# One ring of three PSUM banks for the two softmax attention cores of an eight-sublayer kernel

## What is computed

```python
# layer 0: 16 heads of 32. The last 16 context rows are "compressed" (DCA): own key and value
# projections, and a softmax of their own beside that over the other 496 rows
out = softmax(q k_main^T * s) v_main + DCA_WEIGHT * softmax(q k_dca^T * s) v_dca
# layer 3: 32 heads of 16, rotary embedding on q and k, one softmax over all 512 rows
w = softmax(einsum('bhqd,bhkd->bhqk', q, k) * scale); attn = einsum('bhqk,bhkd->bqhd', w, v)
```

## Time and profile before

| what | value |
|---|---|
| median of 3 runs (lowest to highest) | 3214.14 us (3209.91 to 3215.42) |
| time of the profiled execution | 3215.47 us |
| its span in the trace | 3213.7 us |
| layer 0's attention core | 235.8 to 566.0 us of the span |
| layer 3's attention core | 2333.6 to 2757.3 us of the span |
| TensorE matmul, VectorE, ScalarE, GpSimd busy | 77%, 68%, 50%, 35% |

### The profile page before, as it was taken

The page is one execution under the profiler, slowest core; times in us unless marked ns, Lnnn a source line. Parts: engine busy times, 40 slices in busy tenths (PEclk is TensorE's granted clock), DMA queues, the critical chain, the costliest instruction groups (busy, mean ns, idle before and its releaser), DMA issues. The chain is left out here.

```text
span 3213.7 us, 40834 instructions
## 1 busy us (share of the span) xinstructions
PE 2476.1 (77%) x14030; PEld 1185.7 (37%) x14030; DVE 2175.4 (68%) x3403; ACT 1615.9 (50%) x2278; POOL 1121.1 (35%) x807
## 2 busy tenths in 40 slices
PE   2987889799969935676675599937878899797993
PEld 1541333344434311222223477724512222354661
DVE  6655764435357798999996666655578888546664
ACT  2543555154432665555542355535546767433873
POOL 5764666002001235666662222145541000001444
PEclk9987999899979967899886799978979999998996
DMA  3532220230000000000001577743622100212997
GB/s 126 197 151 72 83 83 15 82 112 1 1 4 12 1 0 1 0 0 1 0 0 53 181 241 240 234 131 124 224 99 80 47 21 14 99 47 99 325 305 238
DMA packets 161699, 300.70 MB, mean 94 GB/s; under 512 B 33540, under 2 KB 79376, under 8 KB 159623
## 3 DMA queue, kind: packets, MB, share of 16 engines
q1 hardware_dynamic: 138646, 219.23, 19.6%
q0 software_dynamic: 22896, 79.44, 8.3%
HBM read 206.08 MB, written 92.27 MB: 93 GB/s over the span
## 5 line engine op out<-in xcount | busy, mean ns | idle before, releaser
L1817 DVE TENSOR_REDUCE ac_nmax<-ac_M 128x1 f32<-128x512 f32 (+1 forms) x768 | 496.6, 687 | 148.7 <-PE ac_M L1631 144.3
L1795 ACT ACTIVATE ac_PT<-ac_S 128x1024 f32<-128x1024 f32 x384 | 371.1, 1017 | 158.7 <-PE ac_S L1666 138.9
L3370 POOL TENSOR_TENSOR sc_hc<-sc_h,sc_cs 128x1024 f32<-128x1024 f32 x128 | 300.7, 2357 | 160.4 <-DVE sc_h L3485 96.4
L3485 DVE TENSOR_TENSOR_SCAN sc_h<-sc_dA,sc_dB 128x1024 f32<-128x1024 f32 x128 | 292.1, 2282 | 12.7 <-ACT sc_dA L3451 12.7
L3405 PE MATMUL sc_y<-sc_hc,ident 128*128 128x512 f32 x512 | 258.1, 631 | 18.3 <-DVE x_res L3501 16.1
L3451 ACT ACTIVATE sc_dA<-ss_delta,sc_A 128x511 f32<-128x511 f32 x256 | 166.0, 682 | 29.9 <-DVE sc_h L3485 29.3
L3383 PE MATMUL sc_b<-ss_bc,sc_sel 128*128 128x512 f16 x128 | 54.1, 423 | 156.4 <-DVE sc_dB L3477 124.9
L1631 PE MATMUL ac_M<-KT,QT 64*128 64x512 f16 (+1 forms) x384 | 141.5, 429 | 41.3 <-DVE ac_nmax L1817 24.6
L3456 ACT ACTIVATE sc_cs<-sc_c 128x512 f32<-128x512 f32 x128 | 76.3, 596 | 185.6 <-POOL sc_hc L3370 182.5
L3477 DVE TENSOR_TENSOR sc_dB<-ss_du,sc_b 128x1024 f32<-128x1024 f32 x128 | 156.1, 1220 | 18.9 <-PE sc_b L3383 7.5
L730 DVE SCALAR_TENSOR_TENSOR mo_up16l<-mo_up,mo_up16h 128x1408 f16<-128x1408 f32 (+1 forms) x77 | 112.7, 1464 | 64.0 <-ACT mo_up16h L670 63.9
(11 more groups left out here) (610 smaller groups left out, 6010.5 us busy)
## 6 DMA issues: line engine op xcount, KB each, us to landing
keys_t<-ap_kto SPq DMA_DIRECT2D x32, 512.0 KB, 2.6
queries_t<-ap_qto SPq DMA_DIRECT2D x32, 512.0 KB, 2.7
mo_up<-in_w_gate SPq DMA_DIRECT2D x23, 704.0 KB, 5.1
mo_up<-in_w_up SPq DMA_DIRECT2D x23, 704.0 KB, 6.7
mo_up<-in_exp_up SPq DMA_DIRECT2D x31, 512.0 KB, 6.1
mo_dn<-in_exp_down SPq DMA_DIRECT2D x31, 512.0 KB, 7.5
slot_results_last<-mo_o SPq DMA_DIRECT2D x31, 512.0 KB, 6.0
mo_dn<-in_w_down SPq DMA_DIRECT2D x23, 512.0 KB, 7.1
```

Source lines behind the costliest of these rows:

```text
L1795: nc.scalar.activation(PT[:, n % PTB, :, :], psS[:, 2 * (n % 2):2 * (n % 2) + 2, :], ACT.Exp, scale=SCALE / (SQK * SQK)).then_inc(exp_done, 1)
L1817: last = v.tensor_reduce(out[:, :, 0], sc[:, 0:MAIN], AX.X, ALU.max)
L3370: nc.gpsimd.tensor_tensor(hc[:, m % RC, :, :], h[:, m % RH, :, :], cs[:, m % 2, :].unsqueeze(1).to_broadcast([P, W, S]), ALU.mult).then_in ...
L3485: nc.vector.tensor_tensor_scan(h[:, m % RH, :, :].rearrange("p c s -> p (c s)"), dA[:, m % 2, :, :].rearrange("p c s -> p (c s)"), dB[:, m ...
```

## The change

The bank `ac_x` is gone and `ac_M` has three banks. All that went through `ac_x` or `ac_M` now takes turns in one ring of three: an entry waits for the reader of the entry three before. In layer 0 a group has 22 entries, in TensorE's order (step 2) four maxima, main values turned; (step 3) compressed values turned, two maxima, compressed values (`dca`), two maxima; (step 0) four maxima, rows, sums; (step 1) four maxima, sums turned. In layer 3 it has 18: 16 maxima, rows after step 0's, values turned after step 2's.

With it: `scores_t(n+3)` moves from ahead of `more(n)` to behind it, in both layers. In layer 0 the copies of the compressed values and of the sums to `ac_oT` move from ScalarE (L1766, L1770) to VectorE (`dca_out` between the two pairs of maxima of step 3, `sums_out` behind the maxima of step 0). Transposes wait for their own input and for the ring alone, no longer for the normalisation of the one before. The matmuls on the compressed values get a semaphore of their own, `dca_mm`, so that `pv_done` is raised ahead of them.

```diff
+    NRING = 3
...
-        psS, psM, po, px = ps("S", [P, 4, S]), ps("M", [P, 2, S]), ps("o", [P, S]), ps("x", [P, S])
+        psS, psM, po = ps("S", [P, 4, S]), ps("M", [P, NRING, S]), ps("o", [P, S])
...
         for n in range(0, TU, 2):
-            use += [("max", m) for m in maxima_of(n)] + [("max", m) for m in maxima_of(n + 1)]
+            g, s = n // UPG, n % UPG // 2
+            if g and s == 3 and not rope:
+                use.append(("turned", g - 1, 1))
+            use += [("max", m) for m in maxima_of(n)]
+            if s == TPB - 1 and not rope:
+                use.append(("dca", g))
+            use += [("max", m) for m in maxima_of(n + 1)]
             if n in at_rows:
                 use.append(("rows", at_rows[n]))
-        if rope:
-            use = [x for x in use if x[0] == "max"]
+            if g and s == 0 and not rope:
+                use.append(("sums", g - 1))
+            if g and s == 1 and not rope:
+                use.append(("turned", g - 1, 2))
+            if g and s == 2:
+                use.append(("turned", g - 1, 0))
...
         for i, x in enumerate(use):
-            ring[x] = (i % 2, use[i - 2] if i >= 2 else None)
+            ring[x] = (i % NRING, use[i - NRING] if i >= NRING else None)
...
             def turned(g, i):
-                if rope:
-                    pe.wait_ge(o_ev, g + 1)
-                    if g:
-                        pe.wait_ge(a_done, g)
-                    pe.wait_ge(rows_ev, min(TG, g + 3))
-                elif i == 2:
+                reader_of(ring["turned", g, i][1])
+                if i == 2:
                     pe.wait_ge(sum_ev, g + 1)
                 elif i == 0:
-                    pe.wait_ge(inv_done, g + 1)
+                    pe.wait_ge(o_ev, g + 1)
                 else:
-                    pe.wait_ge(a_done, g + 1)
+                    pe.wait_ge(d_ev, g + 1)
...
                 scores_t(n + 2)
-                scores_t(n + 3)
                 if g and s == 3 and not rope:
                     turned(g - 1, 1)
                 more(n)
+                scores_t(n + 3)
                 values(n + 1)
                 more(n + 1)
...
                 nc.scalar.activation(oT[:, 0, :], po[:], ACT.Copy).then_inc(o_ev, 1)
-                if not rope:
-                    nc.scalar.activation(oT[:, 1, :], px[:], ACT.Copy).then_inc(d_ev, 1)
-
-            def sums_out(g):
-                act.wait_ge(sum_mm, g + 1)
-                nc.scalar.activation(oT[:, 2, :], px[:], ACT.Copy).then_inc(sum_ev, 1)
...
+            def dca_out(g):
+                dve.wait_ge(dca_mm, g + 1)
+                if g:
+                    dve.wait_ge(ot_T, 3 * g)
+                v.tensor_copy(oT[:, 1, :], bank_of("dca", g)).then_inc(d_ev, 1)
+
+            def sums_out(g):
+                dve.wait_ge(sum_mm, g + 1)
+                if g:
+                    dve.wait_ge(ot_T, 3 * g - 2)
+                v.tensor_copy(oT[:, 2, :], bank_of("sums", g)).then_inc(sum_ev, 1)
...
-                for k in (n, n + 1):
-                    for m in maxima_of(k):
-                        maximum(m)
+                for m in maxima_of(n):
+                    maximum(m)
+                if s == TPB - 1 and not rope:
+                    dca_out(g)
+                for m in maxima_of(n + 1):
+                    maximum(m)
+                if g and s == 0 and not rope:
+                    sums_out(g - 1)
+                if g and s == 1 and not rope:
+                    inverse(g - 1)
```

More of the change, by code:

```diff
@@ L1606, in _ @@
                         pool.wait_ge(pv_done, b * UB)
+                        pool.wait_ge(dca_mm, b * NG)
                         load(b + 1)
@@ L1617, in reader_of @@
             def reader_of(x):
[L1618 to L1621, removed]
+                if x is None:
+                    return
+                kind, g = x[:2]
+                if kind == "max":
+                    pe.wait_ge(max_done, g + 1)
+                elif kind == "rows":
+                    pe.wait_ge(rows_ev, g + 1)
+                elif kind == "dca":
+                    pe.wait_ge(d_ev, g + 1)
+                elif kind == "sums":
+                    pe.wait_ge(sum_ev, g + 1)
+                elif x[2] == 2:
+                    pe.wait_ge(inv_done, g + 1)
+                else:
+                    pe.wait_ge(b_done if x[2] else a_done, g + 1)
             def scores(m):
@@ L1639, in maxima_rows @@
                 pe.wait_ge(m_ready, g + 1)
-                if rope:
-                    if g >= 3:
-                        pe.wait_ge(a_done, g - 2)
-                    if g:
[L1644 to L1650, removed]
+                slot, previous = ring["rows", g]
+                reader_of(previous)
+                out = psM[:, slot, :].bitcast(F16)
                 for j in range(TPB):
@@ L1687, in values @@
                 if not rope and kt == TPB - 1:
-                    if g:
-                        pe.wait_ge(b_done, g)
+                    reader_of(ring["dca", g][1])
+                    last.then_inc(pv_done, NP)
                     for m in range(n + 1 - NP, n + 1):
@@ L1692, in values @@
                             r = 2 * of_unit(m)[2] + i
-                            last = nc.tensor.matmul(px[r * VC:(r + 1) * VC, :], Vd[b % 2][:, g % NG * GH + r, :],
+                            last = nc.tensor.matmul(bank_of("dca", g)[r * VC:(r + 1) * VC, :],
+                                                    Vd[b % 2][:, g % NG * GH + r, :],
                                                     PT[:, m % PTB, i, :], start=True, stop=True)
-                last.then_inc(pv_done, NP)
+                    last.then_inc(dca_mm, 1)
+                else:
+                    last.then_inc(pv_done, NP)
             def sums(g):
@@ L1775, in group_rows @@
                     act.wait_ge(row_in[g % 2], 32 * (g // 2))
-                bank = px[:] if rope else psM[:, ring["rows", g][0], :]
+                bank = psM[:, ring["rows", g][0], :]
                 nc.scalar.activation(mrow[:, g % 2, :], bank.bitcast(F16)[0:NR, 0:S], ACT.Copy).then_inc(rows_ev, 1)
@@ L1798, in _ @@
                     group_out(g - 1)
-                if u == 3 and g and not rope:
-                    sums_out(g - 1)
                 if n - 3 in at_rows:
@@ L1803, in _ @@
             group_out(TG - 1)
-            if not rope:
-                sums_out(TG - 1)
         @block.vector
@@ L1872, in _ @@
             else:
+                sums_out(TG - 1)
                 inverse(TG - 1)
```

36 lines of the change are left out of this document (22 added, 14 removed).

## The result

| | before | after |
|---|---|---|
| median of 4 runs each (lowest to highest) | 3213.51 us (3209.91 to 3215.42) | 3179.61 us (3175.11 to 3182.90) |
| profiled execution, its span | 3215.47, 3213.7 us | 3182.90, 3181.2 us |
| layer 0's core | 330.2 us | 316.1 us |
| layer 3's core | 423.7 us | 408.3 us |
| a steady group of layer 0, of layer 3 | 17.89, 12.41 us | 17.55, 12.01 us |

The ratio is 0.9895, with a 95% interval of 0.9879 to 0.9910: faster by 1.05%, some 34 us. The cores' 14.1 and 15.4 us make 29.5 of the 32.5 us between the two spans; the other 3 lie outside the code that the change touches. That code scatters by more: the stretch between the two cores, which no kernel here changes, takes 1760.5 to 1767.6 us over the 14 profiles.

The account below looks back on a forecast made before the run. Layer 3 was taken as held by a VectorE-TensorE ping-pong over banks, layer 0 by TensorE with gaps. Terms -12.3, -5.8, -2.2, -5.8 and -2.9 sum to -29.0 us: 3215.5 to 3186.5 profiled, 3185 median, range 3158 to 3207.

Parts of the forecast that it names:

- layer 3, steady: Layer 3's groups: a third bank shortens stalls for maxima, 0.41 us a group, -12.3 us.
- layer 3, start: Layer 3's first maxima at the 0.60 pitch (-3.1), small scaling ahead of GpSimd's memset (-2.7): -5.8 us, bounds 0 and -7.
- layer 0, start: Layer 0's 34 maxima at the start go at the reduce's pitch of 0.67 rather than 0.73: -2.2 us.
- layer 0, steady: Layer 0's groups: 17.47 us by the walk, 0.42 less a group over 13.9 groups, -5.8 us.
- layer 0, end: Layer 0's last sums to last product: 5.1 us rather than 6.8, and the 1.22 wait for ScalarE's copy goes, -2.9 us.
- 0.21 for the moved scores: Layer 3's chain: scores_t(n+3) between second maximum and values costs 0.21 us, taken between bounds 0 and 0.43.
- 29.9 groups: Layer 3: the 478 maxima not alone at the start, counted as 29.9 groups gaining 0.41 us each.
- The slower one: Layer 0: GpSimd's additions block sums_out, sums turned 3.2 us late, +45 us, 3230; chance 7%, 11% with other slow turns.
- the product at 402.00: Layer 0: VectorE's product from PSUM took 0.69 us beside GpSimd's additions, evidence against blocked copies.
- The steady parts don't gain: Both layers: moved scores and ring entries eat the third bank, only starts and end gain, -10.9 us, 3203; chance 12%.
- Much more: Both layers: moved scores hide and no stall is left, -61 and -32, 3110; half way 3145; chance 17%.
- ScalarE's two copies: Layer 0: taking two copies of 0.6 us a group off ScalarE is worth nothing, since it waits for TensorE.

Follow-up runs that it names:

- e1: The changed kernel with scores_t(n+3) back ahead of more(n) in both layers: 3138.16 us, ratio 0.9772 to the kernel before.
- e7: The changed kernel with GpSimd's copy of a batch's values in layer 3 cut into four: 3172.85 us, ratio 0.9880 to the kernel before.
- e8: The kernel before with GpSimd's second memset of layer 3's start put behind the output weights: 3208.61 us, ratio 0.9990 to the kernel before.
- e6: The changed kernel with layer 0's copies of compressed values and sums back on ScalarE: 3187.93 us, ratio 0.9923 to the kernel before.

## Why the prediction was right

The predicted 3185.0 us is 5.4 above the median, 3179.61, in the range. The terms, against the two profiled executions:

| term | predicted | measured |
|---|---|---|
| layer 3, steady | -12.3 | -9.1 |
| layer 3, start | -5.8 | -6.3 |
| layer 0, start | -2.2 | -3.2 |
| layer 0, steady | -5.8 | -8.6 |
| layer 0, end | -2.9 | -2.3 |
| sum | -29.0 | -29.5 |

**Layer 3, steady.** The walk gave 12.00 us a group; 12.01 came, with the pauses in the steps it named (0.8 in step 1, 0.2 in others). Its unknown, 0.21 for the moved scores, is the 0.53 - 0.32 of the timeline, and e1 took it away: 0.22 a step. The term is still 3.2 too large, because of the step "29.9 groups": at two of them the batch's copy on GpSimd blocks the scaling, and these grew by 1.9 and 1.8 us, of which the clock is a part. That a faster VectorE would meet that copy elsewhere was said for the start and not looked for in the steady part. e7, without the block, has groups of 12.00 there. The 26 steady groups gave 10.5; the stretch from the first scores to the first product, two groups long, gave 2.5 where 0.8 was counted, and hid a part of the miss.

**Layer 3, start.** Both halves held: the pitch is 0.60, and the scaling ends with the copy (2322.23 + 0.95 against 2321.26 + 1.89). The scaling reads and writes SBUF. The sum rested on rows alone. By the Trainium skill, SBUF — State Buffer, Who interferes with whom, a VectorE instruction in its two-port mode and GpSimd shut each other out for a whole instruction: the traces agree in three places (0.95 and 2.66 under a copy, 4.3 under a memset, 0.17 in e8 alone). That the scaling ran in that mode no trace shows.

**Layer 0, start.** 1.0 more than foreseen, and worth little: the step that failed is taking the gain as one that reaches the end. The profile before had the 13.38 us of TensorE behind GpSimd's weights in plain sight; a stage that ends on another engine's fixed work keeps nothing of what is won ahead of it. From the first scores to the first product of main values it even took 0.7 longer (49.2 us, 48.5 before), which stands in the steady term below.

**Layer 0, steady.** The walk gave 17.47; 17.55 came, and in the order that it named: from the compressed values at 395.13 the sums start 5.51 later (5.49 in the walk), behind a reduce, and are copied at 7.50 (7.43). That is 0.34 a group, 3.4 us over the ten groups that were steady in both kernels. What made the term larger is the two long groups, 5.9 us less, which no step of the prediction mentions: two errors, this one and layer 3's long groups, cancelled. That the sum came out better than its parts is luck.

**Layer 0, end.** The timeline of after, against the earlier trace rows:

```profile
544.78 1.07 PE L1732 MATMUL ac_M<-ac_psum,ac_ones 128*32 128x512 f32 x8 [1.67 <-POOL ac_psum L1591]
...
546.76 0.69 DVE L1883 COPY ac_oT<-ac_M 128x512 f32<-128x512 f32 x1 [2.89 <-PE ac_M L1735]
...
549.38 0.68 DVE L1871 TENSOR_TENSOR ac_tmp<-ac_M,ac_rec 128x512 f32<-128x512 f32 x1
```

From the sums to the end of the last product it is 5.3 us (5.1 foreseen), but the sums still wait, 1.67 us, for GpSimd's additions where ScalarE's copy was: the wait was handed on, not removed. Measured from the same two rows as the prediction's 2.9, the end gives 1.1 (1.5 less work, 0.45 more waiting); the other 1.2 of the table's 2.3 come from the last three groups, which have few or no maxima left.

**The rivals.** The slower one fell: 32 copies of 0.692 us on VectorE, none held by GpSimd, as the product at 402.00 had said. "The steady parts don't gain" fell with the groups. "Much more" did not come, but its condition, the moved scores out of the chain, is e1, which came to 3138 us, 7 below the half way of 3145 that was named. ScalarE's two copies, costed at nothing, cost 0.30 a group where they stood (e6).

## What to carry to other kernels

A ring of buffers and the order of the work that goes through it are one decision: walk the chain from a buffer's release to the next use, and put nothing into it that can stand outside. Here the third bank, with the rest of the change, gave 1.3 us a group, and two matmuls put into that chain in each step took 0.9 of it back. Before counting a gain at a stage's start, look for the next wait that ends on another engine's fixed work, and walk the odd groups (a batch's first) as well as the steady one.

## What was not expected of the hardware

A VectorE scaling of 16 values a partition takes 0.17 us alone, up to 2.7 under a GpSimd copy and 4.3 under a memset; cutting the copy in four gives it a way in, at 2.66 us for the four against 1.90 for the one. TensorE's granted clock was 0.83 in the 10 us around an idle time of 1.57 behind that, and 1.00 in the same window without it: a small stall of VectorE can cost TensorE twice. Whether it does varies: behind 1.68 us of idle time in the kernel before the clock stayed at 1.00, and in other profiles of the same code it fell.

Open are what holds the rows' transfers at layer 0's batch bounds, when TensorE's clock falls behind such a stall, and what the spread weights would give with no piece directly ahead of the loads.
